# Two group-normalized convolutions (3x3, then 5x5) on one core: setup order, first half-image, column ranges of the matmuls, order of work in the fourth step

## The chip, the cores and the metric

The kernel runs on one core of a Trainium2 chip. The metric is the device time of one execution in microseconds (us); the time of before is the median of three runs. TensorE multiplies, VectorE (DVE), ScalarE (ACT) and GpSimd (POOL) do the elementwise work, SyncE (SP) issues most transfers.

## The reference

The input x is 16 images of 32 channels, 128 by 128 pixels, float32. Two residual blocks are computed one after the other:

```
x = x + conv3x3(groupnorm(x), masked weight)      # padding 1
x = x + conv5x5(groupnorm(x), kernel) + bias      # padding 2
```

The group norm has 16 groups of two channels and takes mean and variance over a whole image. The mask of the 3x3 weight keeps a tap of an input channel when its mean absolute value over the output channels exceeds the threshold (and, if 1% or less of the taps pass, keeps all taps that are not zero).

## The kernel before

**Halves and bands.** Each image is two half-images of 64 rows, 32 halves in all. A half has two layouts. In bands (`x_bands` for the first block, `mid_bands` for the second) partition block i (32 channels) holds the 16 rows of band i with one or two rows more at either side; these feed the matmuls. In own rows (`x_own`, `mid`) partition block j holds every fourth row; these fit what comes out of PSUM. `x_bands` has six slots (half h in slot h modulo 6), `mid_bands` three, `mid` five.

**Products.** Weights and normalized pixels are each split into a high float16 part and a low one, and three products are summed in PSUM: high by high, high pixel by low weight, low pixel by high weight. A matmul takes 32 input channels and streams 512 columns, four image rows of 128 pixels. `pairs` has 64 output columns of weights (two vertical taps at once) and eight tiles of the array side by side, `singles` has 32 and sixteen side by side. I call eight pairs or sixteen singles that run side by side a round. For each of the k horizontal taps dx the source starts at column x0 = 2 - k//2 + dx of a padded row of 132 columns, of which the first two and the last two are zero. A pass of `pairs` has 6 rounds for 3x3 and 20 for 5x5; a pass of `singles` has 3 and 5. Three passes of each make a convolution: 27 rounds for 3x3, 75 for 5x5.

**Steps.** Step s does the 3x3 convolution of half s and the 5x5 convolution of half s - 3 (LAG = 3). Steps 0 to 2 have the 3x3 alone (`lead_conv`), steps 3 to 31 both (`whole_step`, one body that TensorE loops over, in the order: 3x3 pairs high, 3x3 pairs low, 5x5 pairs high, 3x3 singles, 5x5 singles, 5x5 pairs low), steps 32 to 34 the 5x5 alone.

**The lead, on VectorE.** `setup3` makes mask, weight scale and split of the 3x3 weight, each operation waiting for the last through a semaphore. Then come statistics of halves 0 and 1 (`stats_in`, four `bn_stats` a half), `set_apart` (aggregate, and lay out for a small matmul that mixes groups), `largest(w5, 1)`, `combine` and `scale_of` (mean and scale). ScalarE writes the high part of half 0 straight from the raw `x_bands` slot 0 (`high3_first`). VectorE meanwhile does `stats_in(2)`, and then `normalize3(0)`, which overwrites slot 0 and so waits for ScalarE (`hi3_done`), and `low3(0)`, the low part. After it: `stats_in(3)`, `set_apart("x", 1)`, `take_conv3(0)` (PSUM scaled plus `x_own` into `mid`), `low3(1)` and so on.

**The queues.** SP issues, in program order: two quarters of w3, bands of halves 0 and 1, w5, bands of 2 and 3, own rows of 0 and 1; then it waits for `mid_made` of half 0, issues own rows of 2, the 16 moves from `mid` to `mid_bands` of half 0, bands of 4, and on to bands of 5, 6 and 7. ScalarE's queue issues the other quarters of w3, then the threshold (one number to 128 partitions), the mixing matrix and the bias. GpSimd issues the 16 moves of half 1 and, behind them, scales w5 (`w5_scaled`) and makes its low part (`w5_split`), with ScalarE making the high part in between (`high_w5`, ahead of the square root of the first `mid` statistics).

**The exchange.** From image 2 on statistics go through DRAM: DVE aggregates (`mv_ready`), ScalarE's queue stores `mv` (`spread_stats`) and loads it to all partitions (`gather_stats`, `mv_in`), DVE computes (`group_stats`, `scale_of`). ScalarE's program is in order: in step 3 it waits in `spread_stats` for `mv_ready` before it takes the 5x5 result out of PSUM (`take_conv5(0)`), and only the drain behind that (L517) lets TensorE start the next 5x5.

The lines of the profile: L873 is the matmul in `pairs`, L891 that in `singles`, L626 `stats_in`, L702 and L730 `normalize3` and `low3` on DVE, L750 `take_conv3`, L758 `stats_out`, L636 `aggregate`, L263 loads of bands, L252 loads of own rows.

Of the kernel before, what the change touches and what calls it, by code (L numbers as in the profile page):

```python
# [43 lines left out]
XB_SLOTS, MB_SLOTS = 6, 3  # L44
PIECES = 2
# [4 lines left out]
def two_blocks(nc, x, w3_dram, thr_dram, w5_dram, bias_dram, mix_dram, out):  # L50
# [7 lines left out]
    with ExitStack() as ctx:  # L58
# [49 lines left out]
        across = sbuf("across", [P, C])  # L108
        turned = sbuf("turned", [P, C])
# [13 lines left out]
        w3_loaded = sem("w3_loaded")  # L123
        w_loaded = sem("w_loaded")
# [124 lines left out]
        def _(sp):  # L249
# [94 lines left out]
        def _(pool):  # L344
# [22 lines left out]
            pool.wait_ge(w5_bounded, 1)  # L367
            nc.gpsimd.tensor_scalar(w5[:, :, :], w5[:, :, :], wfac[:, 1:2], None, ALU.mult).then_inc(w5_scaled, 1)
            pool.wait_ge(w5_hi_made, 1)
            nc.gpsimd.tensor_tensor(s5_lo[:, :, :], w5[:, :, :], s5_hi[:, :, :], ALU.subtract).then_inc(w5_split, 1)  # L370
# [17 lines left out]
        def _(act):  # L388
# [104 lines left out]

            for q in range(Q // 2, Q):
                act.dma_start(w3[quad(q), :, :], w3_dram.rearrange("i a b o -> i (a b) o")).then_inc(w3_loaded, 16)
            act.dma_start(thr[:, :], thr_dram.rearrange("(a o) -> a o", a=1).to_broadcast([P, 1])).then_inc(w3_loaded, 16)
# [55 lines left out]
        def _(dve):  # L552
# [19 lines left out]
            def over_partitions(to, src):  # L572

                own_step(nc.vector.tensor_scalar(across[:, :], ones[:, 0:C], src, None, ALU.mult))
                own_step(nc.vector.transpose(turned[:, :], across[:, :]))
                own_step(nc.vector.tensor_reduce(to, turned[:, :], AX.X, ALU.add))
# [6 lines left out]
            def power_of_two(n):  # L583

                at = slice(n, n + 1)
                over_partitions(total[:, at], bound[:, at])
# [5 lines left out]
                own_step(nc.vector.tensor_scalar(unscale[:, at], power[:, at], 1.0 / (WTOP * PIX), None, ALU.mult))  # L592
# [7 lines left out]
            def setup3():  # L600

                dve.wait_ge(w3_loaded, 16 * (Q + 1))
                own_step(nc.vector.tensor_reduce(score[:, :], w3[:, :, :], AX.X, ALU.add,
                                                 apply_absolute_value=True))
                own_step(nc.vector.tensor_scalar(small[:, 0:1], thr[:, :], 0.0, None, ALU.max))
                own_step(nc.vector.tensor_scalar(mask[:, :], score[:, :], 1.0 / C, small[:, 0:1], ALU.mult, ALU.subtract))
                own_step(nc.vector.tensor_scalar(mask[:, :], mask[:, :], 0.0, None, ALU.is_gt))
                own_step(nc.vector.tensor_scalar(mask0[:, :], score[:, :], 1.0 / C, 0.0, ALU.mult, ALU.is_gt))
                own_step(nc.vector.tensor_reduce(small[:, 1:2], mask[:, :], AX.X, ALU.add))
                over_partitions(small[:, 3:4], small[:, 1:2])  # L610
                own_step(nc.vector.tensor_scalar(small[:, 2:3], small[:, 3:4], 1.0 / (C * T3), 0.01,
                                                 ALU.mult, ALU.is_le))
# [83 lines left out]
            def normalize3(h):  # L696

                dve.wait_ge(x_bands_in[h % XB_SLOTS], 16 * Q * (h // XB_SLOTS + 1))
                if h == 0:
                    dve.wait_ge(hi3_done, 1)  # L700
                v = x_bands[:, h % XB_SLOTS, :, :]
                nc.vector.tensor_scalar(v, v, gmean[:, 0:1], gscale[:, 0:1], ALU.subtract, ALU.mult).then_inc(scaled, 1)  # L702
                dve.wait_ge(scaled, h + 1 - (len(ON_SCALAR) if h else 0))
                q, at = pad_rows(h % 2, 1)
                pad = x_bands[quad(q), h % XB_SLOTS, at, :]
# [19 lines left out]
            def low3(h):  # L725

                dve.wait_ge(hi3_done, h + 1)
                if h:
                    dve.wait_ge(c3_whole, h)
                nc.vector.tensor_tensor(x3_lo[:, :, 2:2 + W], x_bands[:, h % XB_SLOTS, :, :], x3_hi[:, :, 2:2 + W],  # L730
                                        ALU.subtract).then_inc(x3_lo_go, 1)
# [50 lines left out]
            dve.wait_ge(w_loaded, 16 * Q)  # L782
            largest(w5, 1)
# [15 lines left out]
            low3(2)  # L799
            power_of_two(1)  # L800
            nc.vector.drain().then_inc(w5_bounded, 1)
# [11 lines left out]
            stats_out(2)  # L813
            dve.wait_ge(mv_in, 16)
# [48 lines left out]
        def _(pe):  # L863
            def pairs(w, src, k, bank, start=False, every=None):

                for dx in range(k):
                    x0 = 2 - k // 2 + dx
                    for dy in range(1, k):
                        at = dx * k + k - 1 - dy
                        for i in range(Q):  # L870
                            for J in range(2):
                                top = 2 * J + dy
                                ins = nc.tensor.matmul(  # L873
                                    psum[2 * C * J:2 * C * (J + 1), bank + i, :].rearrange("p (a w) -> p a w", a=A),
                                    w[quad(i), at:at + 2, :].rearrange("p t o -> p (t o)"),
                                    src[quad(i), top:top + A * (A - 1) + 1:A, x0:x0 + W],
                                    start=start and dx == 0 and dy == 1, stop=True, skip_group_check=True,
# [5 lines left out]
            def singles(w, src, k, bank, start=False):  # L883

                for dx in range(k):
                    x0 = 2 - k // 2 + dx
                    for i in range(Q):
                        for j in range(Q):
# [3 lines left out]
                                psum[quad(j), bank + i, :].rearrange("p (a w) -> p a w", a=A), w[quad(i), at, :],  # L892
                                src[quad(i), j + dy:j + dy + A * (A - 1) + 1:A, x0:x0 + W],
                                start=start and dx == 0, stop=True, skip_group_check=True, tile_position=(i * C, j * C))
# [130 lines left out]
```

## Time and profile before

| what | us |
| --- | --- |
| median of 3 runs (lowest, highest) | 815.8 (815.01, 816.04) |
| the profiled execution: its time | 814.51 |
| its span, first to last instruction | 812.7 |
| PE busy (matmuls) | 751.7 |
| DVE busy | 615.3 |
| ACT busy | 332.3 |
| POOL busy | 264.6 |

The span is what the rows below tell of; 1.8 us of the profiled execution lie outside it. Busy times of engines that run side by side don't add up. Starts of instructions are from the start of the span. "PEclk" is the clock that TensorE was granted: 1.00 is 2.4 GHz, 0.50 is 1.2 GHz.

### The profile page before, as it was taken

The page shows a single profiled execution, that of the slowest core. Times are in us where ns is not written, and L with a number is a line of the kernel's source. Part 1 is how long each engine was busy: PE and PEld are TensorE (multiplying, and loading weights), DVE is VectorE, ACT ScalarE, POOL GpSimd, SP SyncE. Part 2 cuts the span into 40 slices and gives each one's busy share as a digit, 9 for nine tenths or more (in the row PEclk, how much of TensorE's full clock was granted, in tenths as well). Part 3 has the DMA queues.
Part 4 walks back from the last instruction along what each step waited for, and adds up shares of the span by engine and source line. Part 5 has one row for each costly group of instructions (what it writes and reads, how often), then busy time and mean ns, then how long its engine had stood idle before and what let it go on. Part 6 is the DMA issues. An engine that isn't in the chain of part 4 may idle for free.

```text
span 812.7 us, 67805 instructions
## 1 busy us (share of the span) xinstructions
PE 751.7 (92%) x32292; PEld 503.0 (62%) x32292; DVE 615.3 (76%) x971; ACT 332.3 (41%) x287; POOL 264.6 (33%) x161
## 2 busy tenths in 40 slices
PE   0776689999999999999999999999999999999996
PEld 0442347777666666666666666666666666666564
DVE  6888488787878789797878789697878796663541
ACT  0341316353443436353444436353443436362420
POOL 1050033222334443222334343322334343322360
PEclk9998899999999999999999999999999999999999
DMA  8999489898997979898997979898997956573424
GB/s 186 195 199 224 112 176 230 211 218 201 221 217 178 219 174 222 196 223 194 217 223 164 237 168 227 191 224 196 217 221 186 216 116 163 137 165 86 104 52 103
DMA packets 234176, 150.49 MB, mean 185 GB/s; under 512 B 18656, under 2 KB 227616, under 8 KB 230048
## 3 DMA queue, kind: packets, MB, share of 16 engines
q1 hardware_dynamic: 227168, 144.00, 80.8%
q10 hardware_dynamic: 6272, 4.90, 2.3%
q0 software_dynamic: 704, 1.25, 0.6%
q8 instruction: 10, 0.16, 0.1%
q14 instruction: 22, 0.18, 0.1%
HBM read 75.60 MB, written 33.59 MB: 134 GB/s over the span
## 4 chain that ended last, share of the span: by engine, by line
PE 85%; DMA 5%; SPq 4%; DVE 3%; issue 1%; DVEq 0%; ACT 0%; ACTq 0%
PE psum L873 65%; PE psum L891 20%; DMA x_bands<-x_dram 3%; SPq L271 1%; DVE bn_in L626 1%; SPq L263 1%; SPq L252 1%; DMA mv_scratch<-mv 1%; DMA every_mv<-mv_scratch 1%; DVE x_lo L730 1%; ACT conv_out L477 0%; DVE x_bands L702 0%; SPq L278 0%; DVE mid L750 0%; DVEq L753 0%
## 5 line engine op out<-in xcount | busy, mean ns | idle before, releaser
L376 POOL TENSOR_TENSOR mid<-mid,conv_out 128x512 f32<-128x512 f32 x118 | 241.2, 2075 | 481.5 <-ACT conv_out L477 481.5
L873 PE MATMUL psum<-x_hi,s_hi 32*64 32x512 f16 x6656 | 199.6, 383 | 16.4 <-ACTq L517 8.3
L873 PE MATMUL psum<-x_lo,s_hi 32*64 32x512 f16 x6656 | 197.5, 380 | 6.3 <-DVE x_lo L730 5.3
L873 PE MATMUL psum<-x_hi,s_lo 32*64 32x512 f16 x6656 | 196.5, 377 | 1.4 <-issue 1.4
L873 PEld LDWEIGHTS psum<-x_hi,s_hi 32*64 32x64 f16 x6656 | 107.3, 105 | 98.5 <-ACTq L517 10.2
L873 PEld LDWEIGHTS psum<-x_hi,s_lo 32*64 32x64 f16 x6656 | 127.0, 104 | 58.9 <-issue 2.8
L873 PEld LDWEIGHTS psum<-x_lo,s_hi 32*64 32x64 f16 x6656 | 102.6, 104 | 87.2 <-issue 9.8
L750 DVE SCALAR_TENSOR_TENSOR mid<-psum,unscale,x_own 128x1024 f32<-128x1024 f32 x64 | 79.2, 1278 | 97.8 <-PE psum L891 97.8
L400 ACT ACTIVATE x_hi<-x_bands 128x2304 f16<-128x2304 f32 x31 | 65.7, 2118 | 117.9 <-PE psum L891 117.8
L477 ACT ACTIVATE conv_out<-psum,bias,unscale 128x512 f32<-128x512 f32 x118 | 82.2, 776 | 70.7 <-PE psum L873 62.6
L738 DVE TENSOR_TENSOR x_lo<-mid_bands,x_hi 128x2560 f16<-128x2560 f32 x32 | 92.3, 2885 | 4.1 <-PE psum L873 4.0
L438 ACT ACTIVATE x_hi<-mid_bands 128x2560 f16<-128x2560 f32 x31 | 72.5, 2338 | 52.4 <-PE psum L891 50.7
L445 ACT ACTIVATE mid_bands<-mid_bands,nbias,gscale 128x2560 f32<-128x2560 f32 x31 | 78.2, 2524 | 15.8 <-DVE nbias L693 13.3
L758 DVE BATCH_NORM_STATS2 bn_out<-mid 128x6 f32<-128x512 f32 x128 | 79.1, 681 | 4.4 <-DVE mid L750 0.5
L730 DVE TENSOR_TENSOR x_lo<-x_bands,x_hi 128x2304 f16<-128x2304 f32 x32 | 80.8, 2525 | 0.6 <-ACT x_hi L400 0.2
L891 PE MATMUL psum<-x_hi,s_hi 32*32 32x512 f16 x4096 | 74.7, 380 | 6.6 <-issue 6.6
L393 ACT ACTIVATE root<-gvar 128x1 f32<-128x1 f32 x32 | 6.5, 203 | 181.8 <-DVE gvar L679 161.5
L626 DVE BATCH_NORM_STATS2 bn_in<-x_bands 128x6 f32<-128x512 f32 x128 | 76.8, 664 | 0.7 <-DMA x_bands<-x_dram 0.7
L891 PE MATMUL psum<-x_hi,s_lo 32*32 32x512 f16 x4096 | 74.3, 380 | 0.0
L891 PEld LDWEIGHTS psum<-x_hi,s_hi 32*32 32x32 f16 x4096 | 54.3, 88 | 24.5 <-issue 20.6
L702 DVE TENSOR_SCALAR x_bands<-x_bands,gmean,gscale 128x2304 f32<-128x2304 f32 x29 | 68.7, 2370 | 0.2
L891 PE MATMUL psum<-x_lo,s_hi 32*32 32x512 f16 x4096 | 68.0, 384 | 0.1
(92 smaller groups left out, 348.6 us busy)
## 6 DMA issues: line engine op xcount, KB each, us to landing
x_own<-x_dram SPq DMA_DIRECT2D x128, 256.0 KB, 5.0
mid_bands<-mid SPq DMA_DIRECT2D x372, 80.0 KB, 2.7
out_dram<-mid SPq DMA_DIRECT2D x112, 256.0 KB, 5.4
x_bands<-x_dram SPq DMA_DIRECT2D x96, 288.0 KB, 5.9
x_bands<-x_dram SPq DMA_DIRECT2D x32, 272.0 KB, 6.8
mid_bands<-mid SPq DMA_DIRECT2D x124, 64.0 KB, 2.6
every_mv<-mv_scratch ACTq DMA_DIRECT2D x16, 256.0 KB, 3.8
out_dram<-mid SPq DMA_DIRECT2D x28, 128.0 KB, 2.4
```

The source lines that it names most:

```text
L376: nc.gpsimd.tensor_tensor(m, m, conv_out[:, b, :], ALU.add).then_inc(out_added, 1)
L438: nc.scalar.activation(x5_hi[:, :, 2:2 + W], mid_bands[:, k % MB_SLOTS, :, :], ACT.Copy).then_inc(hi5_done, 1)
L445: nc.scalar.activation(v, v, ACT.Identity, bias=nbias[:, at], scale=gscale[:, at]).then_inc(act_scaled, 1)
L477: nc.scalar.activation(conv_out[:, b, :], psum[:, X5_BANK + b, :], ACT.Identity, bias=bias[:, 0:1], scale=unscale[:, 1:2]).then_inc(conv5_ ...
L626: nc.vector.bn_stats(bn_in[:, h // 2 % 2, h % 2, b, :], rows.rearrange("p a w -> p (a w)")).then_inc(bn_x, 1)
L702: nc.vector.tensor_scalar(v, v, gmean[:, 0:1], gscale[:, 0:1], ALU.subtract, ALU.mult).then_inc(scaled, 1)
L730: nc.vector.tensor_tensor(x3_lo[:, :, 2:2 + W], x_bands[:, h % XB_SLOTS, :, :], x3_hi[:, :, 2:2 + W], ALU.subtract).then_inc(x3_lo_go, 1)
L738: nc.vector.tensor_tensor(x5_lo[:, :, 2:2 + W], mid_bands[:, k % MB_SLOTS, :, :], x5_hi[:, :, 2:2 + W], ALU.subtract).then_inc(x5_lo_go, 1)
L750: nc.vector.scalar_tensor_tensor(mid[:, h % MID_SLOTS, at, :], psum[:, X3_BANK + at.start:X3_BANK + at.stop, :], unscale[:, 0:1], x_own[:, ...
L758: nc.vector.bn_stats(bn_out[:, h % 2, b, :], mid[:, h % MID_SLOTS, b, :]).then_inc(bn_mid, 1)
L873: ins = nc.tensor.matmul(psum[2 * C * J:2 * C * (J + 1), bank + i, :].rearrange("p (a w) -> p a w", a=A), w[quad(i), at:at + 2, :].rearran ...
L891: ins = nc.tensor.matmul(psum[quad(j), bank + i, :].rearrange("p (a w) -> p a w", a=A), w[quad(i), at, :], src[quad(i), j + dy:j + dy + A ...
```

## The change

- **Threshold.** Its load goes ahead of the w3 quarters on ScalarE's queue, under a semaphore of its own.
- **setup3.** The bound of w3 is taken from w3 before the mask; the two sums over partitions (mask count and bound) are done together; subtract-and-compare is one operation; the nine multiplications by the mask are one with a broadcast; the undo factor comes behind the split.
- **SP.** Bands of half 2 are issued ahead of w5.
- **First half.** `normalize3(0)` writes to slot 4 (`SPARE`) and no longer waits for ScalarE; `low3(0)` reads there; both come ahead of `stats_in(2)`. `largest(w5, 1)` moves behind `set_apart("x", 1)`.
- **GpSimd.** The scaling of w5 comes after 8 of the 16 moves, its low part after 12.
- **Step 3 on DVE.** `stats_in(6)` and `stats_in(7)` come ahead of the wait for the exchange, `low3(4)` behind the two aggregates.
- **TensorE.** The centre tap comes first, then outward, and every matmul leaves out the columns where its tap meets only padding: 127 of each 128 columns one tap off centre, 126 two taps off.

```diff
+            load_bands(2)
             for q in range(Q):
                 sp.dma_start(w5[quad(q), :, :], ...).then_inc(w_loaded, 16)
-            load_bands(2)
...
+                if i == 1:
+                    pool.wait_ge(w5_bounded, 1)
+                    nc.gpsimd.tensor_scalar(w5[:, :, :], w5[:, :, :], wfac[:, 1:2], None, ALU.mult).then_inc(w5_scaled, 1)
+                elif i == 2:
+                    pool.wait_ge(w5_hi_made, 1)
+                    nc.gpsimd.tensor_tensor(s5_lo[:, :, :], w5[:, :, :], s5_hi[:, :, :], ALU.subtract).then_inc(w5_split, 1)
...
+            act.dma_start(thr[:, :], ...).then_inc(thr_loaded, 16)
             for q in range(Q // 2, Q):
                 act.dma_start(w3[quad(q), :, :], ...).then_inc(w3_loaded, 16)
-            act.dma_start(thr[:, :], ...).then_inc(w3_loaded, 16)
...
             def over_partitions(to, src):
+                n = src.shape[1]
+                own_step(nc.vector.tensor_copy(across[:, 0:n, :], src.unsqueeze(2).to_broadcast([P, n, C])))
+                own_step(nc.vector.transpose(turned[:, 0:n, :]..., across[:, 0:n, :]...))
+                own_step(nc.vector.tensor_reduce(to, turned[:, 0:n, :], AX.X, ALU.add))
...
             def setup3():
-                dve.wait_ge(w3_loaded, 16 * (Q + 1))
+                dve.wait_ge(w3_loaded, 16 * Q)
                 own_step(nc.vector.tensor_reduce(score[:, :], w3[:, :, :], AX.X, ALU.add, ...))
+                largest(w3, 0)
+                dve.wait_ge(thr_loaded, 16)
                 own_step(nc.vector.tensor_scalar(small[:, 0:1], thr[:, :], 0.0, None, ALU.max))
-                own_step(nc.vector.tensor_scalar(mask[:, :], score[:, :], 1.0 / C, small[:, 0:1], ALU.mult, ALU.subtract))
-                own_step(nc.vector.tensor_scalar(mask[:, :], mask[:, :], 0.0, None, ALU.is_gt))
+                own_step(nc.vector.tensor_scalar(mask[:, :], score[:, :], 1.0 / C, small[:, 0:1], ALU.mult, ALU.is_gt))
...
+                over_partitions(total[:, 0:2], bound[:, 0:2])
...
-                for t in range(T3):
-                    ins = nc.vector.tensor_scalar(w3n[:, t, :], w3[:, t, :], mask[:, t:t + 1], None, ALU.mult)
-                own_step(ins)
-                largest(w3n, 0)
+                own_step(nc.vector.tensor_tensor(w3n[:, :, :], w3[:, :, :], mask[:, :].unsqueeze(2).to_broadcast([P, T3, C]),
+                                                 ALU.mult))
                 power_of_two(0)
                 split_w3()
+                undo_power(0)
...
             def normalize3(h):
-                if h == 0:
-                    dve.wait_ge(hi3_done, 1)
-                v = x_bands[:, h % XB_SLOTS, :, :]
+                v = x_bands[:, h % XB_SLOTS if h else SPARE, :, :]
...
             set_apart("x", 0)
-            dve.wait_ge(w_loaded, 16 * Q)
-            largest(w5, 1)
             dve.drain().then_inc(bank3_go, 1)
             combine(("x", 0))
             scale_of(("x", 0))
-            stats_in(2, range(BANKS))
             dve.wait_ge(zeroed, CLEARED)
             normalize3(0)
             low3(0)
+            stats_in(2, range(BANKS))
             stats_in(3, range(BANKS))
             set_apart("x", 1)
+            dve.wait_ge(w_loaded, 16 * Q)
+            largest(w5, 1)
             take_conv3(0)
...
             stats_out(2)
+            stats_in(2 * LAG, range(BANKS))
+            stats_in(2 * LAG + 1, range(BANKS))
             dve.wait_ge(mv_in, 16)
             group_stats(("x", 2))
             scale_of(("x", 2))
             normalize3(LAG + 1)
             take_conv3(LAG)
             stats_out(LAG)
-            low3(LAG + 1)
-            stats_in(2 * LAG, range(BANKS))
-            stats_in(2 * LAG + 1, range(BANKS))
             aggregate("mid", LAG // 2)
             aggregate("x", LAG, mv_ready)
+            low3(LAG + 1)
...
+            def columns(k):
+                for dx in sorted(range(k), key=lambda d: abs(d - k // 2)):
+                    x0 = 2 - k // 2 + dx
+                    yield dx, x0, max(0, 2 - x0), min(W, W + 2 - x0)
...
-                                    psum[2 * C * J:2 * C * (J + 1), bank + i, :].rearrange("p (a w) -> p a w", a=A),
+                                    psum[2 * C * J:2 * C * (J + 1), bank + i, :].rearrange("p (a w) -> p a w", a=A)[:, :, c0:c1],
                                     w[quad(i), at:at + 2, :].rearrange("p t o -> p (t o)"),
-                                    src[quad(i), top:top + A * (A - 1) + 1:A, x0:x0 + W],
+                                    src[quad(i), top:top + A * (A - 1) + 1:A, x0 + c0:x0 + c1],
```

`singles` is changed in the same way.

## Rows read from the trace of the kernel before

**Rows 1.** The page: busy time by engine, and TensorE in 40 slices of 20.3 us.

```profile
PE 751.7 (92%) x32292; PEld 503.0 (62%) x32292; DVE 615.3 (76%) x971; ACT 332.3 (41%) x287; POOL 264.6 (33%) x161
PE   0776689999999999999999999999999999999996
```

**Rows 2.** Windows: busy of each engine (count), granted clock, DMA share, GB/s.

```profile
113.03:116.45 3.42, 3.42 (x72) 1.71 (x80) 1.76 (x2) 0.00 (x0) 3.42 (x3) 0.50 0.82 176
210.00:310.00 100.00, 100.00 (x4512) 68.65 (x4497) 82.61 (x143) 45.12 (x41) 34.05 (x17) 1.00 0.93 208
```

**Rows 3.** Timeline of TensorE in a steady step: start, length, line, count.

```profile
224.60 1.51 PE L873 MATMUL psum<-x_hi,s_hi 32*64 32x512 f16 x48
228.59 4.56 PE L873 MATMUL psum<-x_hi,s_hi 32*64 32x512 f16 x160
232.96 4.60 PE L873 MATMUL psum<-x_hi,s_lo 32*64 32x512 f16 x160
240.58 1.37 PE L891 MATMUL psum<-x_hi,s_hi 32*32 32x512 f16 x80
241.68 1.36 PE L891 MATMUL psum<-x_hi,s_lo 32*32 32x512 f16 x80
247.40 1.51 PE L873 MATMUL psum<-x_hi,s_hi 32*64 32x512 f16 x48
```

**Rows 4.** The chain that ended last, SP's first band issues; timeline of ScalarE's queue.

```profile
1.64 0.42 SPq L263
2.10 1.76 SPq L263
...
1.66 2.20 ACTq L496 DMA_DIRECT2D thr<-L_conv_threshold_dram  x1
```

**Rows 5.** Transfers issued at 6.25 to 6.80 us: KB, us to landing.

```profile
x_bands<-x_dram SPq DMA_DIRECT2D x1, 272.0 KB, 11.4
```

**Rows 6.** Timeline of the lead, VectorE and ScalarE.

```profile
7.96 0.46 DVE L603 TENSOR_REDUCE score<-w 128x9 f32<-128x288 f32 x1 [6.15 <-DMA thr<-L_conv_threshold_dram]
15.46 4.84 DVE L626 BATCH_NORM_STATS2 bn_in<-x_bands 128x6 f32<-128x512 f32 x8
21.01 0.98 DVE L580 TENSOR_REDUCE bound<-w 128x1 f32<-128x800 f32 x1
24.70 2.31 ACT L407 ACTIVATE x_hi<-x_bands,nbias,gscale 128x2304 f16<-128x2304 f32 x1 [1.19 <-DVE nbias L693]
29.35 2.56 DVE L730 TENSOR_TENSOR x_lo<-x_bands,x_hi 128x2304 f16<-128x2304 f32 x1
35.83 2.48 DVE L750 SCALAR_TENSOR_TENSOR mid<-psum,unscale,x_own 128x1024 f32<-128x1024 f32 x2 [0.73 <-PE psum L891]
```

**Rows 7.** Timeline from 60 us: the first 5x5 on GpSimd, SP's band loads, VectorE.

```profile
61.64 1.71 POOL L370 TENSOR_TENSOR s_lo<-w,s_hi 128x800 f16<-128x800 f32 x1 [0.98 <-ACT s_hi L431]
76.78 5.14 SPq L263 DMA_DIRECT2D x_bands<-x_dram  x8
91.90 0.39 DVE L671 SCALAR_TENSOR_TENSOR product<-every_mv,mix_in 128x128 f32<-128x128 f32 x1 [11.62 <-DMA every_mv<-mv_scratch]
101.82 2.54 DVE L730 TENSOR_TENSOR x_lo<-x_bands,x_hi 128x2304 f16<-128x2304 f32 x1
104.28 4.83 DVE L626 BATCH_NORM_STATS2 bn_in<-x_bands 128x6 f32<-128x512 f32 x8
109.31 0.31 DVE L636 BATCH_NORM_AGGREGATE mv<-bn_in 128x2 f32<-128x48 f32 x1
110.08 2.78 ACT L477 ACTIVATE conv_out<-psum,bias,unscale 128x512 f32<-128x512 f32 x4 [8.09 <-DVE mv L636]
```

**Rows 8.** Timeline of TensorE around the fourth step's start.

```profile
105.16 1.67 PE L873 MATMUL psum<-x_hi,s_hi 32*64 32x512 f16 x48
112.95 6.26 PE L873 MATMUL psum<-x_hi,s_hi 32*64 32x512 f16 x160 [3.46 <-ACTq L517]
```

**Rows 9.** Transfers issued at 81.0 to 82.5 us: KB, us to landing.

```profile
x_bands<-x_dram SPq DMA_DIRECT2D x1, 272.0 KB, 10.0
```

More of the change, by code:

```diff
@@ L44 @@
 XB_SLOTS, MB_SLOTS = 6, 3
+SPARE = 4
 PIECES = 2
@@ L107, in two_blocks @@
         ones = sbuf("ones", [P, P])
-        across = sbuf("across", [P, C])
-        turned = sbuf("turned", [P, C])
+        across = sbuf("across", [P, 2, C])
+        turned = sbuf("turned", [P, 2, C])
         total = sbuf("total", [P, 2])
@@ L123, in two_blocks @@
         w3_loaded = sem("w3_loaded")
+        thr_loaded = sem("thr_loaded")
         w_loaded = sem("w_loaded")
@@ L572, in over_partitions @@
             def over_partitions(to, src):
-                own_step(nc.vector.tensor_scalar(across[:, :], ones[:, 0:C], src, None, ALU.mult))
-                own_step(nc.vector.transpose(turned[:, :], across[:, :]))
-                own_step(nc.vector.tensor_reduce(to, turned[:, :], AX.X, ALU.add))
+                n = src.shape[1]
+                own_step(nc.vector.tensor_copy(across[:, 0:n, :], src.unsqueeze(2).to_broadcast([P, n, C])))
+                own_step(nc.vector.transpose(turned[:, 0:n, :].rearrange("p n c -> p (n c)"),
+                                             across[:, 0:n, :].rearrange("p n c -> p (n c)")))
+                own_step(nc.vector.tensor_reduce(to, turned[:, 0:n, :], AX.X, ALU.add))
             def largest(w, n):
@@ L591, in power_of_two, with undo_power @@
                 own_step(nc.vector.tensor_scalar(wfac[:, at], wfac[:, at], WTOP, None, ALU.mult))
[L592 removed]
+            def undo_power(n):
+                at = slice(n, n + 1)
+                nc.vector.tensor_scalar(unscale[:, at], power[:, at], 1.0 / (WTOP * PIX), None, ALU.mult)
             def split_w3():
@@ L799, in _ @@
             low3(2)
+            over_partitions(total[:, 1:2], bound[:, 1:2])
             power_of_two(1)
+            undo_power(1)
             nc.vector.drain().then_inc(w5_bounded, 1)
@@ L863, in _ @@
         def _(pe):
+            def columns(k):
+                for dx in sorted(range(k), key=lambda d: abs(d - k // 2)):
+                    x0 = 2 - k // 2 + dx
+                    yield dx, x0, max(0, 2 - x0), min(W, W + 2 - x0)
             def pairs(w, src, k, bank, start=False, every=None):
-                for dx in range(k):
-                    x0 = 2 - k // 2 + dx
+                for dx, x0, c0, c1 in columns(k):
                     for dy in range(1, k):
@@ L873, in pairs @@
                                 ins = nc.tensor.matmul(
-                                    psum[2 * C * J:2 * C * (J + 1), bank + i, :].rearrange("p (a w) -> p a w", a=A),
+                                    psum[2 * C * J:2 * C * (J + 1), bank + i, :].rearrange("p (a w) -> p a w", a=A)[:, :, c0:c1],
                                     w[quad(i), at:at + 2, :].rearrange("p t o -> p (t o)"),
-                                    src[quad(i), top:top + A * (A - 1) + 1:A, x0:x0 + W],
-                                    start=start and dx == 0 and dy == 1, stop=True, skip_group_check=True,
+                                    src[quad(i), top:top + A * (A - 1) + 1:A, x0 + c0:x0 + c1],
+                                    start=start and dx == k // 2 and dy == 1, stop=True, skip_group_check=True,
                                     tile_position=(i * C, 2 * C * J))
@@ L881, in pairs, with singles @@
                 return ins
-            def singles(w, src, k, bank, start=False):
-                for dx in range(k):
-                    x0 = 2 - k // 2 + dx
+            def singles(w, src, k, bank):
+                for dx, x0, c0, c1 in columns(k):
                     for i in range(Q):
@@ L891, in singles @@
                             ins = nc.tensor.matmul(
-                                psum[quad(j), bank + i, :].rearrange("p (a w) -> p a w", a=A), w[quad(i), at, :],
-                                src[quad(i), j + dy:j + dy + A * (A - 1) + 1:A, x0:x0 + W],
-                                start=start and dx == 0, stop=True, skip_group_check=True, tile_position=(i * C, j * C))
+                                psum[quad(j), bank + i, :].rearrange("p (a w) -> p a w", a=A)[:, :, c0:c1], w[quad(i), at, :],
+                                src[quad(i), j + dy:j + dy + A * (A - 1) + 1:A, x0 + c0:x0 + c1],
+                                start=False, stop=True, skip_group_check=True, tile_position=(i * C, j * C))
                 return ins
```

18 lines of the change are left out of this document (6 added, 12 removed).

## The prediction

> **What bounds the kernel now.** I read the page first. TensorE is busy for 92% of the span, and its 40 slices show where it isn't: the first five or six (about 110 us) and the last [rows 1]. The windows say the same: from 210 to 310 us TensorE is busy for 100.00 of 100 us at full clock, VectorE for 83, the DMA share is 0.93 [rows 2]. So there are two kernels in one: a steady part in which only shorter matmuls can gain anything, and a lead in which TensorE waits and the chain has to be followed in the timeline.
>
> In the steady part the same instruction starts at 224.60 and at 247.40 us: a step is 22.80 us [rows 3]. The 18 rounds of 3x3 pairs take 228.59 - 224.60 = 3.99 us, 221.7 ns each; 20 rounds of 5x5 pairs 4.37 us, 218.5 ns each; five rounds of 5x5 singles 1.10 us, 220 ns each [rows 3]. Pairs and singles differ by a factor of two in instructions a round and not in time, so the issue doesn't bound them. And in the one window at half clock 72 matmuls, about eight rounds, fill 3.42 us: 0.43 us a round, twice as long [rows 2]. 512 columns at 2.4 GHz are 213.3 ns, at 1.2 GHz 426.7. The streaming of columns bounds a round, plus 5 to 8 ns.
>
> In the lead three places matter. First, bands of half 1: the last of them is issued as the eighth band load, near 6.3 us, and lands 11.4 us later, at 17.7 [rows 5]; VectorE's statistics of halves 0 and 1 end at 15.46 + 4.84 = 20.30 [rows 6]. Second, `take_conv3(0)` at 35.83, on which SP's next loads hang [rows 6]. Third, the start of the fourth step: TensorE has finished the third step at 105.16 and starts the next 3x3, but the 5x5 pairs start only at 112.95, after 3.46 us of idling for ScalarE's L517 [rows 8]. ScalarE was late since it had waited 8.09 us for the aggregate, DVE's L636 at 109.31, and that stood behind `low3(4)` (101.82, 2.54) and the statistics of halves 6 and 7 (104.28, 4.83) [rows 7]. While those wait their turn, DVE had been idle for 11.62 us up to 91.90, for the exchange [rows 7].
>
> **Columns left out.** For 3x3 two of the three taps lose one column in each of four rows: 4 columns of 512, 4/2.4 = 1.67 ns a round. For 5x5 two taps lose 1.67 ns and two 3.33 ns. A pass of 5x5 pairs (4 rounds a tap) saves 8 x 1.67 + 8 x 3.33 = 40 ns, of singles 10 ns; three passes of each: 150 ns. 3x3: 3 x (4 x 1.67 + 2 x 1.67) = 30 ns. All this stands on the path, as TensorE is the bound. From the fourth step's 5x5 on there are 31 5x5 convolutions and 27 3x3: 31 x 0.150 + 27 x 0.030 = 5.46 us. In the first three steps waits swallow it; I count nothing there.
>
> What could take it back is not in the trace: a destination whose rows are broken, and a changed start column. From below: 5x5 passes, which have starts at columns 0 and 4, take 218.5 ns a round, 3x3 passes, which have starts 1, 2 and 3 only, 221.7 [rows 3]. If the 12 of 20 rounds with starts 1 to 3 cost 221.7, the eight others cost 213.7, so where a row starts may be worth up to 8 ns. The change moves start 0 to 2 and leaves 4: 15 rounds of a 5x5 convolution x 8 ns x 31 = 3.7 us at worst, nothing at best. I take a quarter, 0.9, since the taps at 4 may hold most of the gap and the row is shorter too. For the broken destination the nearest row is the same 8 ns: on all trimmed rounds (60 of 75 for 5x5, 18 of 27 for 3x3; 31 x 60 + 27 x 18 = 2346) it would be 18.8 us lost, at best nothing; I take nothing, as the source side is already read in four broken rows at 5 ns over the bare columns. Columns: 4.6 us saved.
>
> **Setup and the first loads.** `setup3` starts at 7.96 when the threshold has landed and hands over at 15.46 [rows 6]. It loses eight small multiplications, an operation and one sum over partitions, some 2 us, and may start earlier. But this is worth nothing: `stats_in(1)` can't end before the last band of half 1 has landed, 17.7, plus its 2.4 us, and it ends at 20.30 now. What decides is that landing. Two things move it. w5 no longer stands right behind half 1, which can give it back up to 0.4 us. The threshold stands first: its issue took 2.20 us on ScalarE's queue, and in just that time SP's second band load took 1.76 us instead of 0.42 [rows 4]; so one queue's slow issue holds up the other's, and now it would hold up SP's w3 and start the bands 1.3 us later. But the engines then have a backlog either way. Landing: between 0.5 earlier and 1.3 later; I take no change. The Trainium skill, "DMA: Bandwidth & Descriptors", section "Issuing engines are not separate DMA queues", says that issuing from several engines at once saves the sequencers' issue time. By that rule SP would not be held up at all and 0 of the 1.3 us could come; the row of this trace shows SP held up, and I go by it for the upper end.
>
> **First half.** `largest(w5, 1)`, 0.98 us, leaves the gap in which DVE waited for the mix anyway (it starts at 21.01); scale is known 0.2 us earlier. ScalarE's high part (2.31 us from 24.70) now runs beside `normalize3(0)`, and `low3(0)` can start at about 27.1 and not 29.35, so TensorE has its low pixels at 29.7 and finishes the first convolution some 2 us earlier. But nobody uses that. DVE still has to do the statistics of 2 and 3 (4.94 us), `set_apart` (0.8) and now `largest(w5, 1)` (1.0) before `take_conv3(0)`: 29.75 + 4.94 + 0.8 + 1.0 = 36.45, where it was 35.83 after 0.73 us of waiting for TensorE [rows 6]. `take_conv3(0)` comes 0.6 us later, and with it SP's chain, since SP waits there. The gain on TensorE is turned into a wait for DVE.
>
> **GpSimd.** Scaling w5 after 8 of 16 moves lets ScalarE get to its square root about 1.3 us earlier, so the low part of half 3 is made 0.5 to 1.9 us earlier. TensorE's third step ends at 105.16, or up to 1.5 us before; the next item shows that this is not used. Moves 13 to 16 land later, but ScalarE reads them only after 93 us.
>
> **Third and fourth step.** The band load of half 7 is the last of the eight issued between 76.78 and 81.92 and lands 10.0 us later, at 91.5 [rows 7, 9]. With SP 0.6 later, 92.15. So `stats_in(6)` fits into the wait, but `stats_in(7)` runs from 92.2 to 94.65, and `group_stats`, at 91.90 now, comes 2.75 us later: a new wait, for a band instead of the exchange. From there DVE's work up to the aggregate loses low3 and both statistics, from 101.82 to just before the first aggregate, 7.2 us: the aggregate ends at 109.62 + 2.75 - 7.2 = 105.2. ScalarE then issues its store and takes the 5x5 result out (0.4 + 2.8, as now) and TensorE's go comes at about 108.6, before TensorE has ended the 3x3 pairs at 105.16 + 4.15 = 109.3 (`low3(4)`, now last, ends at 107.9, when the low pairs want it). So the 5x5 pairs start at 109.3 and not 112.95: 3.65 us. Behind the present gap the clock was granted at half for 3.42 us from 113.03 [rows 2]; with no gap ahead of it that half window, 1.7 us of work, should come back. Lead: 5.35 us. After it DVE and ScalarE are 4.1 us ahead and have slack of several us (DVE 17% idle), so TensorE runs through.
>
> **Sum.** 812.7 - 3.65 - 1.7 - 4.6 = 802.75 us of span, 804.55 for the profiled execution (814.51 before). The median of the runs is 1.3 above that execution: 815.8 - 9.95 = **805.8 us**.
>
> **Rivals.**
> - Columns give nothing (a fixed fetch of a row bounds, not its columns; for it: starts matter at all; against: the time doubles with the clock). Then 815.8 - 5.35 = 810.4.
> - The lead gives nothing. DVE now waits for half 7 in front of everything; up to 109.3 the chain has about 0.6 us of slack, then every us that the last band lands later costs one. A landing 4.3 us later (the threshold's 1.3 and a different packing of the transfers, 10.0 against 11.4 us of flight for the same kind of load [rows 5, 9]) uses up 3.65 us, and the half-clock window comes again. 815.8 - 4.6 = 811.2.
> - Slower: a destination in four broken rows costs each trimmed round. It decides from 9.95/2346 ns above my sum, so from 4.2 ns a round; at the 8 ns of above, 805.8 + 18.8 = 824.6.
> - The change doesn't do what it says: both of the first two, 815.8, or a little above with the 0.6 us.
>
> **How the numbers follow.** My forecast has 0.60 (803 to 808), columns without gain 0.13, lead without gain 0.12, both 0.07, slower 0.08. The range, 802.0 to 811.5, takes in the first three but for their edges. 0.2% of 815.8 is 1.6 us, about what a measurement can tell from no change. Faster 0.85, same 0.07, slower 0.08.
>
> **What would show it.** A steady step of 22.62 to 22.68 us for 22.80; first `take_conv3` near 36.4; `stats_in(7)` ending near 94.7 with DVE idle before it for a band; aggregate ending near 105.2; no idle and no half clock ahead of the fourth step's 5x5. A step of 22.80 or more, or a 5x5 of step 4 at 112 or later, proves the sum wrong.

## The result, and the profile after

The changed kernel takes 806.0 us (median of 4 runs, 805.64 to 806.52; before 815.7 beside it), a ratio of 0.9881 with a 95% interval of 0.9864 to 0.9898: 9.7 us faster, where 805.8 had been forecast. The sum was right to 0.2 us, its terms were not. I follow them in the trace of the changed kernel, whose span is 804.1 us against 812.7. That is 8.6 us and not 9.7, since the profiled execution of before was 1.2 us below the median beside it and the one of after 0.15. Steps are counted from 0 here: the fourth step is the one with s = 4, the fifth the one with s = 5.

The page, busy time by engine:

```profile
PE 748.7 (93%) x32292; PEld 552.8 (69%) x32292; DVE 611.8 (76%) x959; ACT 332.4 (41%) x287; POOL 267.9 (33%) x161
```

The windows (busy us of each engine, granted clock, DMA share, GB/s) show the stretch after the fourth step's start at full clock, where [rows 2] had half, and the steady part as it was:

```profile
107.50:110.90 3.40, 3.40 (x136) 1.94 (x128) 3.40 (x2) 0.00 (x0) 3.40 (x1) 1.00 0.77 197
210.00:310.00 100.00, 100.00 (x4512) 76.88 (x4494) 83.62 (x123) 48.85 (x42) 32.69 (x17) 1.00 0.93 212
```

Timeline of TensorE in a steady step, the rows that answer to [rows 3] (L887 is now the matmul of `pairs`, L904 of `singles`):

```profile
399.69 1.51 PE L887 MATMUL psum<-x_hi,s_hi 32*64 32x512 f16 x48
403.66 4.59 PE L887 MATMUL psum<-x_hi,s_hi 32*64 32x512 f16 x160
408.02 4.62 PE L887 MATMUL psum<-x_hi,s_lo 32*64 32x512 f16 x160
412.57 0.92 PE L904 MATMUL psum<-x_hi,s_hi 32*32 32x512 f16 x48
422.44 1.51 PE L887 MATMUL psum<-x_hi,s_hi 32*64 32x512 f16 x48
```

A merged row carries the shape of its first matmul; the trimmed ones are in its count. The step is 422.44 - 399.69 = 22.75 us, and 22.80 before: 0.05 us saved, where 0.18 less 0.03 had been forecast. Steps vary here between 22.69 and 22.75; from the start of step 8 to that of step 31 the mean is 22.72 (22.75 in a second trace of the same kernel), and 22.80 before. 18 rounds of 3x3 pairs take 3.97 us for 3.99; a pass of 5x5 pairs 4.36 for 4.37; the next one up to the singles 4.55 for 4.53.

The lead, VectorE and the queues, as in [rows 4] and [rows 6], first from the chain that ended last and ScalarE's queue, then from the timeline:

```profile
2.10 1.35 SPq L265
...
0.73 0.41 ACTq L498 DMA_DIRECT2D thr<-L_conv_threshold_dram  x1
1.17 2.28 ACTq L500 DMA_DIRECT2D w<-L_conv_weight_dram  x2
...
16.59 2.47 DVE L635 BATCH_NORM_STATS2 bn_in<-x_bands 128x6 f32<-128x512 f32 x4 [1.27 <-DMA x_bands<-x_dram]
25.88 2.56 DVE L737 TENSOR_TENSOR x_lo<-x_bands,x_hi 128x2304 f16<-128x2304 f32 x1 [1.07 <-ACT x_hi L415]
34.92 2.48 DVE L757 SCALAR_TENSOR_TENSOR mid<-psum,unscale,x_own 128x1024 f32<-128x1024 f32 x2
```

VectorE now waits for the band (1.27 us), as said: the shorter setup is turned into a wait. The band is in at 16.6 and not at 17.7, which is more than the 0.5 us earlier that the forecast allowed. The third and fourth step, as in [rows 7] and [rows 8]:

```profile
85.88 2.47 DVE L635 BATCH_NORM_STATS2 bn_in<-x_bands 128x6 f32<-128x512 f32 x4 [6.53 <-DMA x_bands<-x_dram]
87.90 0.45 PE L904 MATMUL psum<-x_hi,s_hi 32*32 32x508 f16 x4 [4.76 <-issue]
90.99 2.48 DVE L635 BATCH_NORM_STATS2 bn_in<-x_bands 128x6 f32<-128x512 f32 x4 [2.64 <-DMA x_bands<-x_dram]
93.38 0.43 DVE L680 SCALAR_TENSOR_TENSOR product<-every_mv,mix_in 128x128 f32<-128x128 f32 x1
103.40 0.32 DVE L645 BATCH_NORM_AGGREGATE mv<-bn_in 128x2 f32<-128x48 f32 x1
104.17 2.79 ACT L481 ACTIVATE conv_out<-psum,bias,unscale 128x512 f32<-128x512 f32 x4 [1.27 <-DVE mv L645]
106.18 1.53 PE L887 MATMUL psum<-x_lo,s_hi 32*64 32x512 f16 x48 [0.43 <-DVE x_lo L737]
107.53 4.57 PE L887 MATMUL psum<-x_hi,s_hi 32*64 32x512 f16 x160
126.27 1.52 PE L887 MATMUL psum<-x_hi,s_hi 32*64 32x512 f16 x48
```

The idling moved from the exchange (11.62 us) to the two bands (6.53 and 2.64), the aggregate came 5.9 us earlier, ScalarE's wait shrank from 8.09 to 1.27 us, and TensorE's idling of 3.46 us is gone; 0.43 us for `low3(4)` stands in its place. The row at 87.90 is the longest of six gaps in which TensorE stands still in its third step, the first pass through the loop body, 11.8 us together (11.4 before). The profile names nothing that ended them ("issue"), and their cause stays open. The last row starts the fifth step. In the trace of before it is this one:

```profile
133.49 1.50 PE L873 MATMUL psum<-x_hi,s_hi 32*64 32x512 f16 x48
```

So the account of the spans: 133.49 - 126.27 = 7.2 us gained up to the fifth step, and 8.6 - 7.2 = 1.4 us in all that follows it. Forecast: 5.35 and 4.4. In the 1.4 is one step of 23.50 us, from 149.00, with another such gap of TensorE; the second trace of this kernel has none in that place, and there the two parts are 5.9 and 1.7 us.

### The profile page after: what moved, and what is told of

It is laid out like the page before. It is cut to its first block, busy times and chain, and to the rows that moved or that the text cites. A ratio compares the mean times of both kernels' runs of the same rounds, so it can differ in the third digit from the quotient of the medians.

```text
span 804.1 us, 67794 instructions
## 1 busy us (share of the span) xinstructions
PE 748.7 (93%) x32292; PEld 552.8 (69%) x32292; DVE 611.8 (76%) x959; ACT 332.4 (41%) x287; POOL 267.9 (33%) x161
## 4 chain that ended last, share of the span: by engine, by line
PE 86%; DVE 5%; SPq 3%; DMA 3%; issue 1%; DVEq 1%; ACT 1%; ACTq 0%
PE psum L887 66%; PE psum L904 21%; DMA x_bands<-x_dram 3%; SPq L265 1%; SPq L273 1%; DVE bn_in L635 1%; DVE x_lo L737 1%; DVE bn_out L765 1%; DVE mid L757 1%; DVEq L760 1%; SPq L280 0%; ACT conv_out L481 0%; ACT x_hi L411 0%; DVE x_bands L709 0%; DVE mid L868 0%
## 5 line engine op out<-in xcount | busy, mean ns | idle before, releaser
L380 POOL TENSOR_TENSOR mid<-mid,conv_out 128x512 f32<-128x512 f32 x118 | 244.6, 2103 | 471.1 <-ACT conv_out L481 471.1
L887 PE MATMUL psum<-x_hi,s_hi 32*64 32x508 f16 (+2 forms) x6656 | 200.2, 381 | 13.2 <-ACTq L521 4.8
L887 PE MATMUL psum<-x_lo,s_hi 32*64 32x508 f16 (+2 forms) x6656 | 197.6, 379 | 3.8 <-DVE x_lo L737 2.8
L887 PE MATMUL psum<-x_hi,s_lo 32*64 32x508 f16 (+2 forms) x6656 | 198.1, 377 | 0.6 <-issue 0.6
L887 PEld LDWEIGHTS psum<-x_hi,s_hi 32*64 32x64 f16 x6656 | 130.4, 105 | 70.8 <-issue 9.5
L887 PEld LDWEIGHTS psum<-x_hi,s_lo 32*64 32x64 f16 x6656 | 149.7, 104 | 36.3 <-issue 3.5
L887 PEld LDWEIGHTS psum<-x_lo,s_hi 32*64 32x64 f16 x6656 | 108.5, 104 | 78.4 <-issue 9.8
L904 PE MATMUL psum<-x_hi,s_hi 32*32 32x508 f16 (+2 forms) x4096 | 74.0, 377 | 6.2 <-issue 6.2
L904 PE MATMUL psum<-x_hi,s_lo 32*32 32x508 f16 (+2 forms) x4096 | 73.9, 378 | 0.0
L904 PEld LDWEIGHTS psum<-x_hi,s_hi 32*32 32x32 f16 x4096 | 53.2, 88 | 24.2 <-issue 20.0
L904 PE MATMUL psum<-x_lo,s_hi 32*32 32x508 f16 (+2 forms) x4096 | 67.1, 381 | 0.8 <-issue 0.8
```

The lines of the kernel that those rows point to most:

```text
L380: nc.gpsimd.tensor_tensor(m, m, conv_out[:, b, :], ALU.add).then_inc(out_added, 1)
L887: ins = nc.tensor.matmul(psum[2 * C * J:2 * C * (J + 1), bank + i, :].rearrange("p (a w) -> p a w", a=A)[:, :, c0:c1], w[quad(i), at:at + ...
L904: ins = nc.tensor.matmul(psum[quad(j), bank + i, :].rearrange("p (a w) -> p a w", a=A)[:, :, c0:c1], w[quad(i), at, :], src[quad(i), j + d ...
```

## The experiments

Twelve kernels ran in three groups of four, each group on one chip beside the kernel before (816.4, 816.9 and 816.5 us there). I compare ratios to it. The interval of each is about 0.2% to either side, 1.6 us. "The changed kernel" with one part altered is meant throughout, unless said otherwise.

The expectations name four theories. COLUMNS: a trimmed round is shorter by its columns, as forecast. PIECES: a source row costs by the pieces of 16 bytes that it touches. REORDER: the new order in step 3 alone makes the gain of the lead, as forecast. SPREAD: the other edits of the lead carry a good part of it.

**The changed kernel once more**, `after_again`.

> The changed kernel unchanged, beside the runs with one part put back. Both theories: 0.988 of the kernel before. Its trace also shows how much landings of the first bands (last band of half 1 at 16.57 us in the first trace of the changed kernel, 17.74 before) move from run to run.

Measured: 806.2 us, 0.9866 (0.9846 to 0.9886). Its fourth step's 5x5 starts at 108.81 us and its fifth step at 127.55; the last band of half 1 was in at 16.7. Two traces of one kernel that receive this band within 0.2 us of each other are thus 1.3 us apart by the fourth step (107.53 and 126.27 above).

**All columns back**, `full_columns`.

```diff
-                    yield dx, x0, max(0, 2 - x0), min(W, W + 2 - x0)
+                    yield dx, x0, 0, W
```

> The changed kernel with all 128 columns of each row in every matmul again, centre tap still first. Theory COLUMNS (the forecast's: a trimmed round is shorter by its columns, 0.18 us a step, and something else in the change gives 0.1 us back): a step of 22.90 us or more, total some 5 us above the changed kernel. Theory PIECES (a source row costs by the 16-byte pieces it touches, so most trimmed rounds saved nothing): a step of 22.80 us, total 1.5 to 2.5 us above the changed kernel, 807.5 to 808.5.

Measured: 808.2 us, 0.9898 (0.9878 to 0.9919), 0.2 to 0.3% above the changed kernel with overlapping intervals. That speaks against COLUMNS, which wanted 5 us. Its step is not even constant. Four rows of the timeline, with nothing in the program different between them:

```profile
194.88 0.62 PE L887 MATMUL psum<-x_hi,s_hi 32*64 32x512 f16 x16
331.64 1.52 PE L887 MATMUL psum<-x_hi,s_hi 32*64 32x512 f16 x48
...
399.82 0.40 PE L887 MATMUL psum<-x_hi,s_hi 32*64 32x512 f16 x8
...
603.92 0.42 PE L887 MATMUL psum<-x_hi,s_hi 32*64 32x512 f16 x8
```

All four are starts of steps. The six steps from 194.88 to 331.64 take 22.79 us in the mean, the nine from 399.82 to 603.92 take 22.68. From step 8 to step 31 the mean is 22.72, as in the trace of the changed kernel: in this execution, the fastest of six, the left-out columns can't be seen at all. A gain of 0.05 to 0.08 us a step can't be told from this.

**Only the new order of taps and the left-out columns, in the kernel before**, `before_trimmed`.

> The kernel before with only the new order of taps and the left-out columns. COLUMNS: 815.7 - 5 = 811. PIECES: step 22.72 instead of 22.80, 815.7 - 2.2 = 813.5. If the lead gains depend on shorter matmuls, lower than either.

Measured: 813.6 us, 0.9968 (0.9952 to 0.9984): 2.6 us, between 1.3 and 3.9. Its step is 22.75. Together with the run above, the columns are worth some 1 to 3 us, not 4.6. This run also has the new order of taps, so its 2.6 us are the two together; of the 3.1 us between the spans (812.7 and 809.6) 1.5 lie ahead of the fifth step, where the last band of half 1 had landed 2 us earlier with the same order of loads.

**Rows of pixels without padding**, `aligned_rows`: the left-out columns make padding needless, so a row is 128 float16 at a pitch of 256 bytes.

```diff
-    PITCH = W + 4
+    PITCH = W
...
-                    x0 = 2 - k // 2 + dx
-                    yield dx, x0, max(0, 2 - x0), min(W, W + 2 - x0)
+                    x0 = dx - k // 2
+                    yield dx, x0, max(0, -x0), min(W, W - x0)
...
-                nc.scalar.activation(x3_hi[:, :, 2:2 + W], x_bands[:, h % XB_SLOTS, :, :], ACT.Copy).then_inc(hi3_done, 1)
+                nc.scalar.activation(x3_hi[:, :, 0:W], x_bands[:, h % XB_SLOTS, :, :], ACT.Copy).then_inc(hi3_done, 1)
```

(and so wherever `2:2 + W` stood; the memsets of the padding columns are gone)

> The changed kernel with the padding columns gone and a row pitch of 128 float16 (256 bytes): every trimmed row then lies in 16 pieces of 16 bytes, not 17 as most do now. PIECES: all rounds at 211.6 to 215 ns, a step about 0.6 us shorter (22.1), total 31 x 0.6 below the changed kernel: 787 to 789. COLUMNS: no change but the saved memsets, 805 to 806. Rival PITCH (rows at a power-of-two pitch collide in some bank): slower than the changed kernel.

Measured: 792.8 us (792.0 to 793.6), 0.9705 (0.9683 to 0.9727). It is the fastest kernel that computes the whole sum, 13 us below the changed kernel. Its timeline:

```profile
417.25 1.48 PE L885 MATMUL psum<-x_hi,s_hi 32*64 32x512 f16 x48
421.14 4.48 PE L885 MATMUL psum<-x_hi,s_hi 32*64 32x512 f16 x160
425.44 4.47 PE L885 MATMUL psum<-x_hi,s_lo 32*64 32x512 f16 x160
439.54 1.48 PE L885 MATMUL psum<-x_hi,s_hi 32*64 32x512 f16 x48
```

A step of 22.29 us; 3x3 rounds 3.89 us/18 = 216.1 ns (221.7 before), 5x5 rounds 4.30/20 = 215.0 (218.5).

**The same alignment of the centre, no columns left out**, `aligned_full`: `PITCH = W + 16`, pixels at column 8, `yield dx, 8 - k // 2 + dx, 0, W`.

> The changed kernel with pixels starting at column 8 of a row of 144 (288 bytes), all 128 columns in every matmul. Only the centre tap's rows then start on a 16-byte boundary; the others start 2 or 4 bytes off and touch 17 pieces. PIECES: centre rounds at 215, all others at 219 to 220, step about 22.8, 807 to 809. A theory by which only the row's start counts and not how many pieces it touches says the same here, and for aligned_rows it says that the taps right of centre (start 1 and 2) stay at 218 to 220. If trimming alone does the work, this is as full_columns.

Measured: 802.4 us, 0.9825 (0.9803 to 0.9848). It was expected to be 1 to 3 us slower than the changed kernel and is 4 us faster, so the expectation failed:

```profile
421.52 1.49 PE L886 MATMUL psum<-x_hi,s_hi 32*64 32x512 f16 x48
425.44 4.54 PE L886 MATMUL psum<-x_hi,s_hi 32*64 32x512 f16 x160
429.81 4.54 PE L886 MATMUL psum<-x_hi,s_lo 32*64 32x512 f16 x160
444.12 1.49 PE L886 MATMUL psum<-x_hi,s_hi 32*64 32x512 f16 x48
```

A step of 22.60. The two edits help each other: with all columns, the aligned centre and pitch bring 5.8 us (802.4 for 808.2); with columns left out, where alignment reaches the taps left of the centre too, 13 us (792.8 for 806.0).

The starts of all matmuls in 24 steady steps, averaged by tap, give ns from one round of 5x5 pairs to the next (without the rounds at a switch to or from `singles`):

```
kernel          taps in the order of the program; source start, columns      ns a round
before          0/128  1/128  2/128  3/128  4/128           0 and 4: 215 and 219 in turn; 1, 2, 3: 217 to 224
after           2/128  2/127  3/127  2/126  4/126           128 and 127 columns: 217.5 to 224; 126: 212 and 218 in turn
aligned_full    8/128  7/128  9/128  6/128  10/128          215, 220, 219, 218, 218
aligned_rows    0/128  0/127  1/127  0/126  2/126           216, 216, 216 to 217, 212.5, 212.5
```

With a pitch of 264 bytes a row's start moves by 8 bytes against a 16-byte grid from row to row: hence "in turn". Aligned rows cost 215 to 216, others up to 224; 126 columns save 3.3 ns against 128 where the row doesn't touch a seventeenth piece, and 127 columns save nothing in any kernel. In `aligned_full` the pitch is the same for all taps and only the start differs, 215 for 220, so the start of a row costs time by itself, whatever the pitch. The last round before the switch to `singles` differs too: 386 ns before, 418 after, 324 in `aligned_rows`. That is why that one pass is longer after the change than before.

**Shorter rows**, `narrow_rows`: as `aligned_rows`, with `c0 + 120` for the end of all taps but the centre.

> The kernel with aligned rows, off-centre taps cut to 120 columns (eight or so columns of each row are left out of the sum). Taps left of centre read columns 0 to 119, 15 pieces of 16 bytes; taps right of centre start at 1 or 2 and touch 16. COLUMNS: 480/2.4 + 2.3 = 202.3 ns for all off-centre rounds. PIECES: left as that, right up to 213 ns.

Measured once: 769.0 us, a step of 21.51. As it leaves out a part of the sum, only its rounds are compared. The off-centre rounds took, in order, 205 to 206 (source start 0, destination 1), 205 to 209 (start 1, destination 0), 202 (0, 2) and 204 to 207 ns (2, 0). So PIECES as I had put it is wrong too: sixteen pieces don't cost 213 when only 120 columns are asked for. Columns do count; a surcharge of 2 to 9 ns comes on top, smallest for even starts and few pieces, and what sets it exactly stays open. The grid of 16 bytes describes the rounds of these kernels; what in the chip makes it costly is not shown.

**Step 3's old order on VectorE**, `old_step3`.

```diff
             stats_out(2)
-            stats_in(2 * LAG, range(BANKS))
-            stats_in(2 * LAG + 1, range(BANKS))
             dve.wait_ge(mv_in, 16)
...
             stats_out(LAG)
+            low3(LAG + 1)
+            stats_in(2 * LAG, range(BANKS))
+            stats_in(2 * LAG + 1, range(BANKS))
             aggregate("mid", LAG // 2)
             aggregate("x", LAG, mv_ready)
-            low3(LAG + 1)
```

> The changed kernel with the fourth part of the lead put back: stats_in(6) and stats_in(7) behind low3(4), both ahead of the aggregates. Theory REORDER (the forecast's): this alone is the lead gain, 5.35 us above the changed kernel, with the wait on L521 and the half clock back. Theory SPREAD: the earlier first half and GpSimd's order carry 2 us of the lead gain, so this costs 3.5 us or less.

Measured: 812.9 us, 0.9952 (0.9936 to 0.9968), 6.75 us above `after_again`. Timeline of TensorE and ScalarE, and the window with the half clock:

```profile
112.33 3.21 PE L887 MATMUL psum<-x_hi,s_hi 32*64 32x512 f16 x56 [4.63 <-ACTq L521]
116.17 1.08 PE L887 MATMUL psum<-x_hi,s_hi 32*64 32x508 f16 x16
...
109.45 2.79 ACT L481 ACTIVATE conv_out<-psum,bias,unscale 128x512 f32<-128x512 f32 x4 [8.35 <-DVE mv L645]
...
110.40:117.20 6.80, 4.87 (x96) 2.30 (x104) 4.29 (x4) 1.84 (x3) 6.80 (x4) 0.50 0.76 167
```

The wait of [rows 8] is back, 112.33 for 108.81, and behind it half clock for 6.8 us, 4.9 of them with TensorE at work, where before had 3.4. REORDER stands. Its 6.75 us are not clear of 5.35 with intervals of 1.6 us on each kernel, and the spans of the two traces are 5.9 apart; but SPREAD's 3.5 is ruled out. What TensorE loses to the clock after a gap is 1.7 us in before and 2.4 here.

The rows at 112.33 and 116.17 are nine rounds apart, all at half clock: 3.84 us, 426.7 ns a round, just what 512 columns take at 1.2 GHz. These rows are not aligned, and five of the nine rounds have 127 columns a row. So at half clock there is no surcharge to be seen, and leaving out the 128th column saves nothing there either.

**w5 in front again**, `w5_earlier` (SP issues w5, then the bands of half 2).

> The changed kernel with w5 ahead of the bands of half 2 again. REORDER: within 0.4 us of the changed kernel. SPREAD: the last band of half 1 lands up to 1.2 us later and the total is about 1 us above.

Measured: 806.6 us, 0.9870 (0.9848 to 0.9891). No difference; the last band of half 1 was in at 16.6.

**The first half as before**, `old_first_half` (the edits of `normalize3(0)`, `low3(0)`, `stats_in(2)` and `largest(w5, 1)` put back).

> The changed kernel with the first half as before: normalize3(0) in place and behind stats_in(2), largest(w5, 1) early. REORDER (the forecast's sum for this part: take_conv3(0) 0.6 us earlier than in the changed kernel): 0 to 0.6 us below the changed kernel, as TensorE's earlier first convolution is used by nobody. SPREAD: 1 us or more above it.

Measured: 809.2 us, 0.9910 (0.9892 to 0.9929), 3.0 us above. Neither theory had the reason. The timeline shows one:

```profile
23.09 0.99 DVE L586 TENSOR_REDUCE bound<-w 128x1 f32<-128x800 f32 x1 [3.33 <-DMA w<-L_conv_kernel_dram]
...
37.90 2.48 DVE L759 SCALAR_TENSOR_TENSOR mid<-psum,unscale,x_own 128x1024 f32<-128x1024 f32 x2 [0.71 <-PE psum L906]
```

With w5 behind the bands of half 2, an early `largest(w5, 1)` waits 3.33 us for it, ahead of `combine`.

**Both put back**, `old_first_half_w5`.

> The changed kernel with both the first half and SP's order as before, so that largest(w5, 1) finds w5 landed. If the 3 us that the old first half cost alone came from its wait for w5 (landed at 23.1 us, behind the bands of half 2), this is 0 to 0.6 us below the changed kernel, as the forecast's sum says; if they came from the order of low3(0) and the statistics, 2 to 3 us above.

Measured: 805.6 us, 0.9869 (0.9851 to 0.9888). The 3 us are gone; the first half's new order and SP's new order together bring nothing.

**The threshold behind w3 again**, `thr_later`.

> The changed kernel with the threshold's load behind the quarters of w3 again (its own semaphore kept). Forecast: 0 to 1.3 us faster, if the threshold in front held up SP's first loads; within 0.5 us if the hold-up of both queues near 2 us comes whatever is issued, as the changed kernel's trace has it too.

Measured: 806.9 us, 0.9884 (0.9865 to 0.9904). No difference beyond the intervals. Both queues are held up near 2.1 us here too, SP's issue for 1.20 us and the threshold's for 1.64. The trace shows one thing more: the threshold landed only at 10.45 us, where it lands between 4.3 and 4.8 when it is issued first, and `setup3` stood waiting for it. The last band of half 1 came late as well, at 18.2, which hid that wait; the fourth step's 5x5 starts at 110.14.

**GpSimd's work on w5 last**, `pool_last`.

> The changed kernel with GpSimd's two operations on w5 behind all 16 moves again. Forecast: the low part of half 3 made 0.5 to 1.9 us later, not used further on: within 0.5 us of the changed kernel. Rival: TensorE's first pass through the new body is bound by its code arriving block by block, and every us that it starts later ends it later: 1 us or more above.

Measured: 805.5 us, 0.9879 (0.9858 to 0.9900). No difference.

## Why the prediction was right

**Columns left out: the step that failed, in its size.** Forecast 4.6 us, measured 1.4 and 1.7 in the spans, 2.6 (1.3 to 3.9) in `before_trimmed`, and barely separable from nothing in `full_columns`. "The streaming of columns bounds a round, plus 5 to 8 ns" took the 5 to 8 ns for a constant. They are a surcharge that depends on where rows start, and trimming keeps or raises it: 127 columns save none of their 1.67 ns, 126 save their 3.3 only in half of the rounds (212 for 215), about 1 in the other (218 for 219). I had seen that starts matter, and bounded it at 8 ns for the one tap whose start moves. The bound itself was worked out from rounds that can't be compared: within the same 5x5 pass of before, starts 1 to 3 take 219 to 220 ns and not 221.7, starts 0 and 4 take 217 and not 213.7. I did not ask what the surcharge would do in the taps whose start stays: there it is as large as what is trimmed. The clock argument (time doubles at half clock) was read too coarsely. At half clock a round is 427 ns in before and in `old_step3`, less than twice the 218.5 at full clock: the columns double and the surcharge is gone. So it is not a fixed number of TensorE's cycles, and what bounds a round of unaligned rows at full clock is not the columns alone.

**Third and fourth step: right in mechanism, undersized.** In numbers of the forecast, of `after_again` and of the first trace of the changed kernel: `stats_in(7)` starts at 92.2, 92.25 and 90.99, the aggregate ends at 105.2, 104.99 and 103.7, the 5x5 starts at 109.3, 108.81 and 107.53. The half clock behind the gap is gone. That the second trace meets the forecast so closely is in part chance, as the first shows. What the forecast had wrong is on TensorE: it took the third step to end at 105.16 and said that an earlier end would not be used. With the wait gone the 3x3 pairs are what the 5x5 waits for, and an earlier end is used: the fourth step starts at 102.75 in the first trace and 104.47 in the second, and the 5x5 4.8 and 4.3 us later. No run shows what moves that end; `pool_last` shows that GpSimd's order doesn't. The isolated value is 6.75 us for 5.35 forecast; of the difference, 0.7 is that half clock covers 4.9 us of work without the reorder and not 3.4, the rest lies within the intervals.

**Setup and first loads: nothing of their worth is shown**, as said, but by a wrong reading. No kernel puts the old `setup3` back. All edits but the columns and step 3 together are worth 1.3 us by the ratios of `before_trimmed` (0.9968) and `old_step3` (0.9952), inside the intervals. SP's second band load was held for 1.76 us beside the threshold's slow issue [rows 4], and I took the one for the cause of the other. With the threshold in front its own issue takes 0.41 us, and whatever either queue issues near 2 us is held instead (SP's second band load for 1.35 us, one of the w3 quarters on ScalarE). The rule of the Trainium skill that I had weighed against it, "DMA: Bandwidth & Descriptors", section "Issuing engines are not separate DMA queues", says only that issuing from several engines saves sequencer time. For the threshold's place the 0 us that I drew from it comes out nearer than my reading; the hold of both queues at one time, which every trace here shows, is not in that rule. The last band of half 1 landed between 15.7 and 18.2 us in the traces of before, after and the twelve kernels, and the order of the loads doesn't sort them (15.7 and 17.7 are both of the old order).

**First half: right in what bounds it, late in one number.** From the known scale to `take_conv3(0)` VectorE takes 11.8 us (23.17 to 34.92), and 11.2 before: the 0.6 us that were forecast. That it came at 34.92 and not 36.45 (the terms add up to 36.49) is for the most part the band's landing, 1.2 us earlier. `old_first_half_w5`, no different from the changed kernel, agrees with the forecast that TensorE's earlier first convolution is used by nobody.

**GpSimd: nothing, as said** (`pool_last`, 805.5 us).

**The rivals.** "Columns give nothing" was nearly the case (0.13 given to it), and it was hidden by a lead that gave 1.9 us more in one trace and 0.6 in the other. The broken destination costs nothing that can be seen: in `aligned_rows` a round with 127 columns takes 216 ns, as one with 128. That the total was met to 0.2 us is luck: two errors cancelled in part (the span was forecast at 802.75 and came out at 804.1), and the median of before lies further above its profiled execution than that of after. Taken by terms, the columns were two to three times too large.

## What to carry to other kernels

Before counting columns, compare rounds of the same length whose rows start in different places: if they differ, a surcharge of alignment is there, and a trimmed row may save nothing until its start is put right. Rounds at half clock, where a trace has some, are a second check: here they showed the bare columns. When a change makes padding needless, take the padding out: here that brought 13 us, more than all of the change. And when two edits only work as a pair (a later load and a later use), put both back together, or the experiment measures its own new wait.

## What the runs showed of the hardware that I had not expected

- TensorE with eight tiles side by side and sources of four rows: 215 to 216 ns a round for 512 columns when rows start on a 16-byte boundary, 217 to 224 when not; 127 columns a row cost as much as 128. At half clock 427 ns, aligned or not.
- The same program can change its round time in the middle of an execution (22.79 to 22.68 us a step in `full_columns`). With a pitch that is a multiple of 16 bytes no trace shows this: from step 5 on, every step is 22.60 in `aligned_full` and 22.29 in `aligned_rows`.
- In this kernel a GpSimd operation on two tensors held a small VectorE operation on two tensors until its own end: in the timeline of the changed kernel GpSimd's L374 runs from 58.02 for 1.71 us, and VectorE's L664, 0.17 us otherwise, takes 1.55 from 58.21. In `after_again` it is 1.58 us, and in before VectorE's L687, 0.16 us otherwise, takes 1.48 beside the same GpSimd operation.

```profile
58.02 1.71 POOL L374 TENSOR_TENSOR s_lo<-w,s_hi 128x800 f16<-128x800 f32 x1
58.21 1.55 DVE L664 SCALAR_TENSOR_TENSOR product<-members,ones 128x8 f32<-128x8 f32 x1
```
